# Mixture-of-experts block on one core: the TensorE expert loop unrolled into five tested tiles, with identity transposes ahead of its first work

## The reference

```python
x = hidden_states                                   # (4, 1024, 512) float32
x = x + attn(layernorm(x))                          # linear attention, 16 heads of 32
x = x + moe(layernorm(x))

# attn: q, k, v = h @ W.T + b;  qp, kp = elu(q)+1, elu(k)+1
#       out = (qp @ (kp^T v)) / (qp . sum(kp) + 1e-6);  out @ o_w.T + o_b
# moe:  gates = softmax(h @ gating_w), 8 experts, the best 2 per token,
#       weights normalised over the two; each expert takes the first 1280 rows (capacity)
#       y = relu(rows @ w1[e] + b1[e]) @ w2[e] + b2[e]   (512 -> 2048 -> 512)
#       each token gets the weighted sum of its two experts' y
```

## Time and profile before

| what | value |
|---|---|
| median of 3 runs | 2091.21 us (2087.82 to 2092.98) |
| profiled execution | 2088.93 us, span 2087.2 us |
| mean granted clock of PE | 0.991 of full speed |
| PE busy | 97% of the span |
| DVE, ACT, POOL busy | 45%, 29%, 20% |
| chain that ended last | 90% PE |

### The profile page before, as it was taken

One profiled execution on the slowest core, in us unless ns is written; L12 is line 12 of the kernel. 1 busy time (PEld: TensorE's weight loads), 2 busy tenths in 40 slices (PEclk: granted clock), 3 DMA queues, 4 the chain that ended last, 5 costly groups with the idle time before them and its releaser, 6 DMA issues.

```text
span 2087.2 us, 28714 instructions
## 1 busy us (share of the span) xinstructions
PE 2020.4 (97%) x10096; PEld 1750.4 (84%) x10097; DVE 931.5 (45%) x1766; ACT 597.7 (29%) x890; POOL 422.6 (20%) x472
## 2 busy tenths in 40 slices
PE   7999999997999999999999999999999999999996
PEld 6788888876779989998889888888998888888995
DVE  5455556566832463345233533342346235235332
ACT  3333333321321341234122422231224124124221
POOL 1012123335621211221121121120211111110221
PEclk9999999998999999999999999999999999999998
DMA  6212122154202440244022421330234124224221
GB/s 181 75 52 81 61 81 68 50 172 126 73 22 41 111 116 20 40 111 116 21 41 50 141 55 31 120 89 7 40 72 140 34 70 136 40 63 139 45 40 20
DMA packets 114878, 156.10 MB, mean 75 GB/s; under 512 B 28032, under 2 KB 60928, under 8 KB 114816
## 3 DMA queue, kind: packets, MB, share of 16 engines
q1 hardware_dynamic: 93216, 112.13, 16.9%
q0 software_dynamic: 21600, 43.16, 11.4%
HBM read 113.15 MB, written 42.10 MB: 74 GB/s over the span
## 4 chain that ended last, share of the span: by engine, by line
PE 90%; DVE 3%; issue 2%; ACT 1%; POOL 1%; DMA 1%; SPq 0%; ACTq 0%; DVEq 0%; POOLq 0%
PE bank L1287 28%; PE bank L1289 28%; PE bank L1288 28%; PE bank L1306 2%; PE bank L1295 2%; PE bank L1469 1%; PE bank L1457 1%; PE bank L1444 1%; POOL slot_table L528 0%; DMA xr<-_attn_hidden_states_dram 0%; DVE et_lo L850 0%; DVE w_lo L838 0%; ACT w_hi L629 0%; ACT h L659 0%; DMA xb<-_attn_hidden_states_dram 0%
## 5 line engine op out<-in xcount | busy, mean ns | idle before, releaser
L864 DVE CAST h_hi<-h 128x512 fp32r<-128x512 f32 x320 | 142.1, 444 | 841.1 <-ACT h L659 841.0
L659 ACT ACTIVATE h<-bank,b_cur 128x512 f32<-128x512 f32 x320 | 220.1, 688 | 993.9 <-PE bank L1289 993.7
L1287 PE MATMUL bank<-et_hi,w_hi 128*128 128x384 f32 (+1 forms) x1280 | 457.5, 357 | 12.6 <-issue 7.9
L1289 PE MATMUL bank<-et_hi,w_lo 128*128 128x384 f32 (+1 forms) x1280 | 456.3, 356 | 0.0
L1288 PE MATMUL bank<-et_lo,w_hi 128*128 128x384 f32 (+1 forms) x1280 | 455.0, 356 | 0.0
L1289 PE MATMUL bank<-w_hi,h_lo 128*128 128x512 f32 x1072 | 420.9, 393 | 0.0
L1287 PE MATMUL bank<-w_hi,h_hi 128*128 128x512 f32 x1072 | 420.6, 392 | 0.0
L1288 PE MATMUL bank<-w_lo,h_hi 128*128 128x512 f32 x1072 | 420.2, 392 | 0.0
L514 POOL DMA_INDIRECT out_dram<-ys,tab_s x80 | 132.8, 1660 | 1018.7 <-ACT ys L646 1000.4
L1287 PEld LDWEIGHTS bank<-et_hi,w_hi 128*128 128x128 f32 x1280 | 241.4, 189 | 42.7 <-issue 14.3
L1288 PEld LDWEIGHTS bank<-et_lo,w_hi 128*128 128x128 f32 x1280 | 241.3, 189 | 24.8
(11 more groups left out here) (186 smaller groups left out, 2214.8 us busy)
## 6 DMA issues: line engine op xcount, KB each, us to landing
w_raw<-L_ffn_w_dram SPq DMA_DIRECT2D x128, 512.0 KB, 3.4
xb<-_attn_hidden_states_dram SPq DMA_DIRECT2D x32, 256.0 KB, 2.7
xr<-_attn_hidden_states_dram SPq DMA_DIRECT2D x32, 256.0 KB, 3.3
out_dram<-x SPq DMA_DIRECT2D x32, 256.0 KB, 3.5
normed<-x1n SPq DMA_DIRECT2D x32, 256.0 KB, 3.5
normed<-zrow SPq DMA_DIRECT2D x1, 2048.0 KB, 8.2
out_dram<-zrow SPq DMA_DIRECT2D x1, 2048.0 KB, 13.3
b_cur<-L_ffn_b_dram SPq DMA_DIRECT2D x8, 256.0 KB, 3.0
```

The costliest lines, as they stand in the source:

```text
L659: nc.scalar.activation(h32[:, mm % 2, :], h_bank[mm % 2][:], ACT.Relu, bias=b1_cur[:, mm:mm + 1]) \
L864: ve_.tensor_copy(h_hi[:, mm % 4, :], h32[:, mm % 2, :]).then_inc(h_split_hi, 1)
L1287: mm_(out_, lh, rh, start=(first and c == 0), stop=False)
L1289: ins = mm_(out_, ll, rh, start=False, stop=(last and c == n - 1))
```

## The change

PE alone is touched. There are three edits.

1. In the expert loop the two inner loops go. Five bodies stand in a row, for 4, 3, 3, 4 and 3 blocks, each under a test of its own.
2. `warm` issues matmuls of the 128x128 identity with itself into a bank that is not yet in use: 6 before step 0 and 10 ahead of the v product of tile 0.
3. The waits for the split matrices v and k leave the head of the products. In tile 0 the product waits ahead of each half of the matrix for that half; later tiles don't wait for them.

```diff
+            def warm(times):
+                for _ in range(times):
+                    mm_(bank[6][:, 0:P], ident[:], ident[:], start=True, stop=True)
+
-            def product(out_, left, right, n, first=True, last=True):
+            def product(out_, left, right, n, first=True, last=True, matrix=None):
                 for c in range(n):
+                    if matrix is not None and c % 2 == 0:
+                        pe.wait_ge(st_lo, 2 * matrix + c // 2 + 1)
...
+            warm(6)
             for t in range(STEPS):
                 v = tile_at(t, VK)
+                if v == 0:
+                    warm(10)
                 if v is not None:
...
-                    pe.wait_ge(st_lo, 2)
...
-                    product(bank[2][:], rows_, lambda k: (whi["v"][:, k, :], wlo["v"][:, k, :]), KC).then_inc(v_full, 1)
+                    product(bank[2][:], rows_, lambda k: (whi["v"][:, k, :], wlo["v"][:, k, :]), KC,
+                            matrix=0 if v == 0 else None).then_inc(v_full, 1)
...
-                    pe.wait_ge(st_lo, 4)
...
-                    product(bank[1][:], rows_, lambda k: (whi["k"][:, k, :], wlo["k"][:, k, :]), KC).then_inc(k_full, 1)
+                    product(bank[1][:], rows_, lambda k: (whi["k"][:, k, :], wlo["k"][:, k, :]), KC,
+                            matrix=1 if v == 0 else None).then_inc(k_full, 1)
...
             with pe.Fori(0, E) as e:
                 fours, threes, _, before = tiles_of(pe, e)
-                with pe.Fori(0, 2) as t:
-                    with pe.If(t < fours):
-                        tile(e, before + t, BT)
-                with pe.Fori(0, TPE) as t:
-                    with pe.If(t < threes):
-                        tile(e, before + fours + t, BT - 1)
+                with pe.If(fours > 0):
+                    tile(e, before, BT)
+                with pe.If(threes > 0):
+                    tile(e, before + fours, BT - 1)
+                with pe.If(threes > 1):
+                    tile(e, before + fours + 1, BT - 1)
+                with pe.If(fours > 1):
+                    tile(e, before + 1, BT)
+                with pe.If(threes > 2):
+                    tile(e, before + 2, BT - 1)
```

## The result

The changed kernel takes 2194.2 us (median of 4 runs, 2191.31 to 2200.04) against 2090.0 us: a ratio of 1.050 (95% interval 1.0487 to 1.0512), slower by 5%. The forecast was 2180 us, with a range of 2146 to 2208. The profiled execution spans 2189.5 us, 102.3 us more than the one before.

The account below looks back on a forecast made before the run. PE, 97% busy, was taken to bound the kernel. Profiled 2088.9 us, +79 at expert borders, +13 for half clock and -2.5 for warming and split waits gave 2178; the median, 2.3 above, 2180 us, range 2146 to 2208.

Parts of the forecast that it names:

- What bounds the kernel: PE busy 97% of the span; the loop edit can win only 12.6 us idle before first-layer matmuls, mostly at tile borders.
- the 3.6 us at the first border as a fetch: First border (615.95 to 623.76): 3.6 us beyond failed tests is PE fetching code that isn't on the engine.
- 3712 instructions aren't kept: Expert loop's five bodies exceed what PE keeps, so each jump over a body or back to the head fetches code.
- The price of a fetch, 3.6 us each: Expert loop: each jump to absent code costs 3.6 us; 26 fetches, borders 91.3 us against 12.4 now, +79.
- fetches in a chain cost more: Expert loop: the next jump waits behind the following block's fetch, 0.9 us for 16 of 26 fetches, 2195 us; chance 0.15.
- The base inside an expert, 1.5: Inside one expert, T (last transpositions to next tile's first matmul) starts from 1.5 us, in place of 2.4 between experts.
- A failed test at 0.4: Expert loop: a failed test without a loop round it costs 0.4 us, where today's costs 0.9.
- The clock, +13: Matmuls at half clock behind eight border gaps of 3 us or more, 2.0 us each, less 3.2 now: +13.
- Warming and split waits, -2.5: Start of the first stage: v product starts earlier, the transposition after it at 14.71 instead of 17.12: -2.5 us.
- The first jump of expert 0: Start of expert 0, skipping body 1: one failed test, one fetch; 6.4 us from last transpositions to first matmul, 2.7 idle.
- The code is kept: Rival: expert loop's code stays on the engine, only first jumps to bodies 1, 4 and 5 fetch; 2089 us, chance 0.06.
- jumps are cheap: Rival: first border's 3.6 us was something else at loop entry; about 2 us stay at borders; 2075 us, chance 0.08.

Follow-up runs that it names:

- the dead code: Kernel before plus identity matmuls that never run at the outer loop's end: 100, 300 or 744 instructions; 2094.9, 2122.4 and 2157.9 us, one run each.
- the front edits alone: Edits 2 and 3 (warming, split waits) with the expert loop of before: 2087.6 us against 2090.8, ratio 0.9988.
- The counted loop: Kernel before with edits 2 and 3 and one inner loop run once per tile, holding two bodies under tests: 2082.0 us, ratio 0.9956.

## Why the prediction was right, and where its sizes were off

- *What bounds the kernel; the 3.6 us at the first border as a fetch.* Right: two instruction packets start in that border and none in four later ones, and the dead code has the same jumps with no fetch at 100 instructions and fetches at 300 and 744.
- *3712 instructions aren't kept.* Right: 139 packets against 37, and "issue" gaps at 10 of 19 borders. The rows ahead left the size open; the runs put the limit between 1716 and 1916.
- *The price of a fetch, 3.6 us each.* This is the term that was mis-sized: by T less the floor, as in the sum, the borders came to 107.8 us where 91.3 were worked out. A single one was about right: T = 5.64 with one, less the base of 2.4, is 3.2, and the first border taken the same way gives 3.1 to 3.6 in the eight executions with the inner loops. In a chain each further jump adds (27.06 - 5.64) / 4 = 5.4 us, test included, where 4.0 stood in the sum. That is the rival "fetches in a chain cost more": it named 16 further fetches at 0.9 us, 2195 us in all, and 2194.2 was measured. I had given it 0.15, so the forecast held by its range, and this rival was nearer in size and in cause. Its first half is borne out: the following block is fetched as well. In the gap of five jumps the packets start in pairs some 5 us apart (two each from 2008 to 2010, 2013 to 2015 and 2019 to 2021, none between). That the next jump waits for that second packet isn't shown, as both of each such pair start within 0.6 us.
- *The base inside an expert, 1.5.* Too high: T was 3.67 inside expert 1 (skipping body 4), so 3.67 - 0.4 - 3.2 leaves almost nothing. Inside expert 3, 9.5 was expected for T and 9.5 measured: that is luck, the low base and the dearer chain cancel.
- *A failed test at 0.4.* It stands: with 100 dead instructions the borders grew by 0.4 to 0.5 us each.
- *The clock, +13.* The stretches at half clock are there behind the large gaps. By T, the work between the borders grew by 10.0, so the sum was about right. How much of the 10.0 is clock alone wasn't taken apart.
- *Warming and split waits, -2.5.* Right: -2.6 at the transposition of tile 1, and -3.2 in the medians of the front edits alone. The -3.0 at the end of the stage is one pair of executions; that end scatters by 3 us with either first stage (612.95 to 616.41 with the edits, 615.95 to 619.03 without).
- *The first jump of expert 0.* 6.4 expected for T, 5.67 measured.
- *The code is kept* and *jumps are cheap* both fell, at the first border where they were to decide.

What the prediction didn't see is the bound behind the borders: it took the 12.4 us of failed iterations as winnable by the loop edit alone. The counted loop shows that 5.6 us come that way, and the rest (9.1 more) only when ACT and DVE give the first activation of a new tile precedence.

## What to carry to other kernels

Before a loop's bodies are written out to save branches, count the instructions from its head to its end: on PE a loop of some 1700 ran from what the engine holds, one of 1900 fetched again behind every expert that had run both of its bodies. Above that, each jump over a body costs 3 to 5 us, which outweighs a failed iteration of 0.9 by far; a counted loop round one body of each kind had neither cost. And when idle time at a border is pure "issue", ask what is late next: here ACT's first activation stood 2 us behind and took back nearly half of what the closed borders gave.

## What the runs showed of the hardware that I had not expected

Jumps to absent code don't add up evenly: 3.2 us for one alone, 5.4 for each further in a row. A loop that spans 1916 instructions, less than the 2048 that the Trainium skill's page "Runtime: NRT & Kernel Launch" gives for PE, was fetched again in part: 31 packets and some 30 us more than before, in one run, and only where both of its bodies had run. A hint at the loop's head hid one fetch whole (T 5.64 to 3.01) and took one packet from each of the seven jumps back. And a wait of 1.87 us was enough ahead of a stretch at half clock (0.50 granted from 767.8 to 771.2 in the counted loop), where waits of as much as 2.0 at the borders of the kernel before had not been followed by one.
